# Layer 0's attention loop in another order: single scores beside maxima's products, products with v in two pieces, a spread finish, roots on VectorE

## The reference

```python
# layer 0, attention: 16 heads of 8
qkv = x @ W_attn + b_attn
att = einsum('bhtd,bhsd->bhts', q, k) / sqrt(8) + alibi_causal_mask   # -inf above the diagonal
y = einsum('bhts,bhsd->bhtd', softmax(att), v)
return y @ W_proj + b_proj
# layer 0, FFN: x normalised again, scaled by its largest magnitude, times ternary weights
xq = clip(xn * 128 / gamma, ...);  return (xq @ w_q) * (gamma * beta / 128)
# layer 1: linear attention with RoPE in chunks, and an FFN with a gate over 8 experts
xn = layernorm(x)
```

## Time and profile before

| | us |
|---|---|
| median of 3 runs | 527.51 (521.96 to 528.45) |
| the profiled execution | 526.21 |
| its span, first to last instruction | 524.4 |

### The profile page before, as it was taken

The page is one execution under the profiler, slowest core; times in us unless marked ns, Lnnn a source line. Parts: engine busy times, 40 slices in busy tenths (PEclk is TensorE's granted clock), DMA queues, the critical chain, the costliest instruction groups (busy, mean ns, idle before and its releaser), DMA issues. The chain is left out here.

```text
span 524.4 us, 10855 instructions
## 1 busy us (share of the span) xinstructions
PE 423.6 (81%) x4220; PEld 192.8 (37%) x4220; DVE 352.3 (67%) x584; ACT 273.4 (52%) x599; POOL 183.5 (35%) x277
## 2 busy tenths in 40 slices
PE   6796788887887877777779689796789868987995
PEld 3253212222232222222233254243446534644764
DVE  5778758788787977787625468498644964586361
ACT  1565367777767777767746702345603340344331
POOL 3013413445230313232210106566623851486220
PEclk9998769999999999999979779798989998999999
DMA  7643060424202002020000003131020301120000
GB/s 230 195 113 70 28 216 0 150 69 165 70 3 69 2 22 49 2 68 2 3 3 0 2 36 131 54 122 63 2 81 21 123 12 71 41 101 2 2 22 21
DMA packets 19094, 31.92 MB, mean 61 GB/s; under 512 B 2544, under 2 KB 7120, under 8 KB 18724
## 3 DMA queue, kind: packets, MB, share of 16 engines
q1 hardware_dynamic: 19044, 31.23, 18.6%
HBM read 13.20 MB, written 8.06 MB: 41 GB/s over the span
## 5 line engine op out<-in xcount | busy, mean ns | idle before, releaser
L1103 DVE TENSOR_REDUCE pmax<-PS 128x8 f32<-128x1024 f32 x144 | 171.9, 1222 | 50.2 <-PE PS L597 32.0
L1414 ACT ACTIVATE prob<-PS 128x512 f32<-128x512 f32 (+1 forms) x320 | 159.9, 552 | 74.1 <-PE PS L665 70.9
L1558 POOL TENSOR_SCALAR_AFFINE_SELECT prob<-prob 128x512 f32<-128x512 f32 x64 | 39.9, 635 | 180.3 <-ACT prob L1414 180.3
L665 PE MATMUL PS<-q_op,k_op 55*128 55x512 bf16 (+3 forms) x384 | 61.6, 341 | 43.7 <-ACT prob L1414 41.3
L683 PE MATMUL PS<-prob,vaug 128*16 128x512 f32 (+3 forms) x768 | 83.1, 523 | 0.0
L597 PE MATMUL PS<-k_op,q_op 52*128 52x128 bf16 (+3 forms) x576 | 58.6, 280 | 10.0 <-DVE pmax L1103 5.4
L665 PEld LDWEIGHTS PS<-q_op,k_op 55*128 55x128 bf16 x384 | 18.4, 94 | 124.8 <-ACT prob L1414 108.7
L1596 POOL TENSOR_TENSOR xn<-state,c_sb 128x512 f32<-128x512 f32 x28 | 32.1, 1146 | 71.8 <-DVE state L1284 63.1
L792 PE MATMUL PS<-xnT,w_sb 128*128 128x512 f32 x80 | 45.6, 672 | 11.7 <-DVE by_sin L1251 11.7
L1284 DVE TENSOR_TENSOR state<-PS,xn 128x512 f32<-128x512 f32 x28 | 19.3, 688 | 40.7 <-PE PS L875 27.8
L1579 POOL TENSOR_TENSOR qr<-qr,turned 128x512 f32<-128x512 f32 x32 | 42.9, 1359 | 5.0 <-DMA turned<-by_sin 5.0
(11 more groups left out here) (182 smaller groups left out, 536.3 us busy)
## 6 DMA issues: line engine op xcount, KB each, us to landing
turned<-by_sin SPq DMA_DIRECT2D x80, 128.0 KB, 2.0
k_op<-k_scr SPq DMA_DIRECT2D x14, 220.0 KB
q_op<-q_scr SPq DMA_DIRECT2D x14, 208.0 KB
...
```

What stands on the lines that cost most here:

```text
L665: last = mm(PS[:, (GH * s + h) % ST_BANKS, at:at + nn], k_op[rows, slot, h // 2, P * j:P * j + P], q_op[rows, slot, h // 2, P * i0:P * i0 ...
L1103: vec.tensor_reduce(pmax[:, of_pair, at:at + step * (TPS - 1) + 1:step], both.rearrange("p a (b c) -> p a b c", c=P), AX.X, ALU.max).then_ ...
L1414: sca.activation(prob[:, s % P_SLOTS, h, 0:UNIT_W[u]], PS[:, k % ST_BANKS, 0:UNIT_W[u]], ACT.Exp).then_inc(s_exp, 1)
L1558: po.affine_select(out=blk, in_=blk, compare_op=ALU.is_ge, fill=0.0, base=0, pattern=[[0, GH], [1, P]], channel_multiplier=-1).then_inc(s_ ...
```

## The change

1. The loop's half steps take one head's score at a time, and beside each, on the other rows of PE, one half of a max item (`max_beside`) where the half step's first item is one. The odd item of a step with three goes to the first half.
2. `pv(s - 1)` is cut in two pieces: the first, without own blocks, after the third score, the second, with the own blocks, after the fourth; only the second waits for POOL.
3. `ROUNDS` has longer rounds (12 products in place of 18 for a head). Own blocks are now in 5 of 9 rounds, and the mask is added by four products of 64 rows by 64 columns of the array, over the own blocks alone. `ROW` shrinks from 6 to 4.
4. ACT copies `yacc` between the third and the fourth exponential of the step after.
5. yt, yT and the first proj go into groups 5 to 7 (`MIDWAY`): steps 42, 45, 49, 52 (yt), 56, 59 (yT) and 68 (proj); proj(1), back, back and xn1T are in steps 71, 72, 73 and 76. `quantise` is in steps 63 and 65.
6. The roots of layer 1's norm are taken on DVE (`inverse_root`: 16 small operations, a first guess by an integer shift and four rounds of Newton's method) in place of ACT's Sqrt, in step 74 and in layer 1's chunk 1.

```diff
-ORDER = [(0, 1, 3, 2), (6, 7, 5, 4)]
-DIAGONALS = {0: ORDER[0], 3: ORDER[1]}
-ROUNDS = [[(i, i, 1, at) for at, i in enumerate(DIAGONALS[0])],
-          [(1, 0, 1, 0), (3, 0, 3, 1)], [(2, 0, 2, 0), (6, 4, 2, 2)],
-          [(i, i, 1, at) for at, i in enumerate(DIAGONALS[3])],
-          [(7, 0, 4, 0)], [(7, 4, 3, 0), (5, 0, 1, 3)], [(5, 1, 4, 0)], [(4, 0, 4, 0)], [(6, 0, 4, 0)]]
-
-ROW = [6, 8]
-ROWS_AT = [0, 6 * TPS]
-
-PLACE = {0: (3, 6), 1: (11, 1), 2: (22, 1), 3: (27, 9), 4: (32, 1), 5: (37, 1), 6: (41, 1), 7: (48, 1), 8: (28, 1)}
+def pv_pieces(segs):
+    j, i0, nn = segs[0]
+    if i0 != j:
+        return [[(j, i0 + m * nn // 2 // P, nn // 2, m * nn // 2)] for m in range(2)]
+    return [[(j, i0 + 1, nn - P, P)], [(j, i0, P, 0)] + [(j1, i1, n1, nn) for j1, i1, n1 in segs[1:]]]
+
+
+PIECES = [pv_pieces(segs) for _, segs in UNITS]
+
+
+
+ORDER = [(3, 2, 0, 1), (5, 6, 4, 7)]
+ROUNDS = [[(3, 0, 4, 0)], [(2, 0, 3, 0), (0, 0, 1, 3)], [(1, 0, 2, 0), (5, 4, 2, 2)],
+          [(7, 0, 4, 0)], [(7, 4, 4, 0)], [(6, 0, 4, 0)], [(5, 0, 4, 0)], [(4, 0, 4, 0)], [(6, 4, 3, 0), (4, 4, 1, 3)]]
+
+OWN = [[at + i - j for i, j, nb, at in pieces if i < j + nb] for pieces in ROUNDS]
+
+ROW = [4, 8]
+ROWS_AT = [0, 4 * TPS]
+
+PLACE = [0, 5, 14, 40, 44, 24, 18, 33, 29]
 NR, NR0 = len(ROUNDS), 3
 NMAX = NR * PAIRS
 MAX_OF = [(p, r) for rs in (range(NR0), range(NR0, NR)) for p in range(PAIRS) for r in rs]
...
-TAIL = [(70, "yt", 0, 0), (71, "yt", 0, 1), (72, "yt", 1, 0), (73, "yt", 1, 1), (74, "yT", 0, 0), (74, "yT", 1, 0),
-        (75, "proj", 0, 0), (75, "proj", 1, 0), (76, "back", 0, 0), (76, "back", 1, 0), (79, "xn1T", 0, 0)]
+TAIL = [(71, "proj", 1, 0), (72, "back", 0, 0), (73, "back", 1, 0), (76, "xn1T", 0, 0)]
+MIDWAY = {(5, 5): ("yt", 0, 0), (5, 11): ("yt", 0, 1), (6, 0): ("yt", 1, 0), (6, 6): ("yt", 1, 1),
+          (6, 12): ("yT", 0, 0), (7, 0): ("yT", 1, 0), (7, 17): ("proj", 0, 0)}
 
 
 def item_stream():
...
+            if (n, u) in MIDWAY:
+                out.append(MIDWAY[n, u])
             if n == NG and u in (13, 15):
                 out.append((("lanes", "spread")[u == 15], 0, 0))
...
-QUANTISE_STEP = [72, 73]
+QUANTISE_STEP = [63, 65]
...
             pe.wait_ge(s_pick, 32)
             pe.wait_ge(s_masks, 16)
 
+            def max_ready(k):
+                _, n, u = ITEMS[k]
+                slot = n % OP_SLOTS
+                pair, r = MAX_OF[u]
+                if n == 0 and r == 0:
+                    for w_, it in enumerate(ITEMS):
+                        if it[0] == "prep" and it[2] // 2 == pair:
+                            used(pe, w_)
+                elif u == 0:
+                    pe.wait_ge(s_op[slot], OP_EACH * (n // OP_SLOTS + (slot > 0)))
+
+
+            def max_piece(k, t, odd):
+                _, n, u = ITEMS[k]
+                slot, ring = n % OP_SLOTS, 3 + 2 * (k % 2)
+                pair, r = MAX_OF[u]
+                i, j, nb, at = ROUNDS[r][t]
+                rows = rows_of(odd, MAX_K)
+                return mm(PS[:, ring + odd, P * at:P * (at + nb)], q_op[rows, slot, pair, P * i:P * i + P],
+                          k_op[rows, slot, pair, P * j:P * (j + nb)], start=(t == 0), stop=(not OWN[r]),
+                          skip_group_check=True)
+
+            def max_done(k, last):
+                _, _, u = ITEMS[k]
+                ring = 3 + 2 * (k % 2)
+                own = OWN[MAX_OF[u][1]]
+                if own:
+                    cols = slice(own[0], own[-1] + 1, max(1, own[-1] - own[0]))
+                    for h in range(2):
+                        for odd in range(2):
+                            rows = slice(HALF * odd, HALF * odd + HALF)
+                            ps = PS[HALF * h:HALF * h + HALF, ring + odd, :].rearrange("p (b c) -> p b c", c=P)
+                            last = mm(ps[:, cols, :], ident_b[rows, rows],
+                                      causal_b[rows, h:h + 1, :].broadcast_to([HALF, len(own), P]),
+                                      start=False, stop=True, skip_group_check=True)
+                last.then_inc(s_item, 1)
+
+
+
+            def max_beside(k, odd):
+                if odd:
+                    used(pe, k - 2)
+                    max_ready(k)
+                for t in range(len(ROUNDS[MAX_OF[ITEMS[k][2]][1]])):
+                    last = max_piece(k, t, odd)
+                if not odd:
+                    max_done(k, last)
+
...
                     last.then_inc(s_item, 1)
                 elif kind == "max":
-                    slot = n % OP_SLOTS
-                    pair, r = MAX_OF[u]
-                    if n == 0 and r == 0:
-                        for w_, it in enumerate(ITEMS):
-                            if it[0] == "prep" and it[2] // 2 == pair:
-                                used(pe, w_)
-                    elif u == 0:
-                        pe.wait_ge(s_op[slot], OP_EACH * (n // OP_SLOTS + (slot > 0)))
-                    for t, (i, j, nb, at) in enumerate(ROUNDS[r]):
+                    max_ready(k)
+                    for t in range(len(ROUNDS[MAX_OF[u][1]])):
                         for odd in range(2):
-                            rows = rows_of(odd, MAX_K)
-                            last = mm(PS[:, ring + odd, P * at:P * (at + nb)], q_op[rows, slot, pair, P * i:P * i + P],
-                                      k_op[rows, slot, pair, P * j:P * (j + nb)], start=(t == 0), stop=(r not in DIAGONALS),
-                                      skip_group_check=True)
-                    for odd in range(2 if r in DIAGONALS else 0):
-                        last = mm(PS[:, ring + odd, :].rearrange("p (b c) -> p b c", c=P), ident_b,
-                                  causal_b.rearrange("p (o c) -> p o c", o=1).broadcast_to([P, TPS, P]),
-                                  start=False, stop=True, skip_group_check=True)
-                    last.then_inc(s_item, 1)
+                            last = max_piece(k, t, odd)
...
-            def pv(s):
+            def pv(s, piece):
                 n, u = divmod(s, NU)
                 b, g = GROUPS[n]
-                half, segs = UNITS[u]
-                pe.wait_ge(s_exp, GH * (s + 1))
-                pe.wait_ge(s_tri, TRI[s])
-                if u in (0, 3):
-                    pe.wait_ge(s_acc, 1 + 2 * n + (u == 3))
-                at = 0
-                for j, i0, nn in segs:
+                half = UNITS[u][0]
+                if piece == 0:
+                    pe.wait_ge(s_exp, GH * (s + 1))
+                    if u in (0, 3):
+                        pe.wait_ge(s_acc, 1 + 2 * n + (u == 3))
+                else:
+                    pe.wait_ge(s_tri, TRI[s])
+                for j, i0, nn, at in PIECES[u][piece]:
                     c0 = P * i0 - SPAN * half
                     for h in range(GH):
                         last = mm(PS[STRIP * h:STRIP * h + VW, 7, c0:c0 + nn], vaug[:, TPB * b + j, g * GH + h, :],
-                                  prob[:, s % P_SLOTS, h, at:at + nn], start=(j == 0),
+                                  prob[:, s % P_SLOTS, h, at:at + nn], start=(j == 0 and piece == 0),
                                   stop=(u in (2, 9)), skip_group_check=True)
-                    at += nn
-                last.then_inc(s_pv, 1)
+                if piece:
+                    last.then_inc(s_pv, 1)
 
             def unit_b(k, part):
 
...
             for s in range(NSTEP + 1):
                 beside = items_of_step(s) if s < NSTEP else ()
                 for half in range(2):
-                    if s < NSTEP:
-                        scores(s, range(GH // 2 * half, GH // 2 * (half + 1)))
-                    for k in (beside[:len(beside) // 2], beside[len(beside) // 2:])[half]:
+                    mine = (beside[:(len(beside) + 1) // 2], beside[(len(beside) + 1) // 2:])[half]
+                    with_scores = s < NSTEP and mine and ITEMS[mine[0]][0] == "max"
+                    for odd in (1, 0):
+                        if s < NSTEP:
+                            scores(s, [GH // 2 * half + 1 - odd])
+                        if with_scores:
+                            max_beside(mine[0], odd)
+                        if s and half:
+                            pv(s - 1, 1 - odd)
+                    for k in mine[1:] if with_scores else mine:
                         item(k)
-                if s:
-                    pv(s - 1)
 
 
             pe.wait_ge(s_exp, GH * NSTEP)
...
+            def inverse_root(t, eps):
+                y, half = rstd[:, t], std[:, t]
+                aux = rstd2[:, t]
+                note(vec.tensor_scalar(half, mv[:, t, 1], eps, -0.5, ALU.add, ALU.mult))
+                link(vec.tensor_scalar(aux, mv[:, t, 1], eps, None, ALU.add))
+                link(vec.tensor_scalar(y.bitcast(I32), aux.bitcast(I32), 1, None, ALU.logical_shift_right))
+                link(vec.tensor_scalar(y.bitcast(I32), y.bitcast(I32), -1.0, float(0x5F3759DF), ALU.mult, ALU.add))
```

(14 more changed lines are left out.)

46 lines of the change are left out of this document (26 added, 20 removed).

## The result

| | before | after |
|---|---|---|
| median, us | 527.98 (521.96 to 529.21) | 536.26 (534.24 to 539.23) |
| ratio | | 1.021 (95%: 1.015 to 1.027) |
| the profiled execution; its span | 526.21; 524.4 | 536.07; 534.3 |

The change makes the kernel 2.1% slower. The forecast was 511.2 us with a range of 500 to 525, and 0.06 for slower; it was wrong.

What follows compares the result with a forecast made beforehand. No engine is full; two chains of transfers in each group of ten steps limit the loop's gain. Terms -1.6 - 2.5 - 1.8 - 0.8 + 1.9 - 11.9 - 1.0 + 2.7 = -15.0 from 526.2 gave 511.2 us, range 500 to 525.

Steps and rivals of the forecast that it cites:

- loop order: Attention loop, single scores beside maxima and product in two pieces: free full step 2.5 us against 2.76, 0.35 us a group gained.
- the second item's ring: Attention loop step, second max item's buffer from one reduction's end to the next, first piece inside: 2.52 us a step.
- u5 to u8: Sixth to ninth steps of each group of ten in the attention loop: claimed nothing gained, PE only standing longer, 1.8 us.
- Load chain: From a group's sixth step to the next group's first maxima, transfers then operand loads: stays 12.24 us, PE stands 1.8.
- half chain: Second and third steps of each group, mrow copy and four small transfers: together stay about 6.0 us, gain 0.
- The moved items: yt, yT, proj and quantise moved from the last group into steps 42 to 68: +1.9 us in sum, four of them 0.
- The last group: Steps 70 to 79 and the loop's end: 41.5 us down to 29.6, gain 11.9; at upper ends 32, gain 9.5.
- Start: First steps of the loop: -1.6 us in step 1 and -2.5 in steps 3 to 9.
- The clock behind the loop: After the attention loop: with half of PE's stand before 295.97, less time at the lower clock, -1.0 us.
- B: Rival: PE's longer stands before loads lower the clock once or twice more in the loop; 523 us, chance 0.16.
- C: Rival: the clock falls at the load stand in every group; 538 us, slower than before; chance 0.06.
- D: Rival: second item's chain in a loop step longer than worked out, steps of 3.05 us; 521 us, chance 0.08.

## Why the prediction was wrong, by its own steps

**The step that failed first: loop order.** It put the second item's ring at 2.52 us with the piece in it, and set that against the old step, 2.76, as a gain. Measured is 0.06 + 0.32 + 0.56 + 0.45 + 1.22 = 2.61. That small miss is not the point; two others are. The masks belong in this ring, and I had put them to PE's busy time alone (0.15 to 0.2 us): 0.24 us where they cover two blocks (204.98 to 205.22 in the rows below). The steps with own blocks take 2.75 to 2.86. And the number that mattered was not asked for: the ring without the piece. It is 0.56 shorter, DVE becomes the bound, and the steps u5 to u8 take 2.45 to 2.68. I compared the new step with the old one, and never the edit with its absence. Forecast for the order was a gain; measured, the pieces' place alone costs 3.0 us in steps 10 to 39, 6.6 in 40 to 69 and 18 of the whole.

```profile
204.98 0.30 PE L616 MATMUL PS<-masks_sb 64*64 64x256 bf16 x4
205.08 0.60 ACT L1490 ACTIVATE prob<-PS 128x512 f32<-128x512 f32 x1 [0.32 <-PE PS L713]
205.22 0.41 PE L732 MATMUL PS<-prob,vaug 128*16 128x128 f32 x8
```

**What hides the loop's gain.** Load chain and half chain were the forecast's reason for 0.35 us a group. In the kernel after the load chain bound nothing (0.3 us of k_op waits where I had 1.8 in each group); the steps with own blocks, at 2.75 to 2.86, were no faster than before. In the kernels with fast steps the stands did come, 0.9 to 1.8 us in step 19, but with the product at the end the loop gained 4.2 us in three groups in spite of them, not 0.35 a group. So this part was right in kind and too strong.

**The moved items.** "Within the chains' slack: 0" for four of them, +1.9 in all. Measured 8.7 in the kernel after, and 4.2 in the kernel before. With the load chain not binding there was no slack in the kernel after. And the price of one is more than its 1.03 us of PE: it stands in front of scores and takes a ring buffer. In the kernel without pieces the same items cost 6.2.

**The last group** was right in mechanism: PE's stand for xn 1.79 us (forecast 1.7), the whole 27.7 to 29.3 us in the five kernels with single scores and at most 3.4 us at half clock there (29.6), 31.8 in the profile shown, with 10.2 us at half clock: step 76 took 6.94 in place of 5.03 (4.7). But against 36 to 41 us without the moved items, what it gives is what the loop paid.

**Start**: -4.1 forecast, +0.8 measured, with 27 us at half clock in it (20 before), which the forecast had let stay. Part is the pieces again: with 17 us at half clock in each, 41.2 with them between the scores, 37.7 to 39.3 without, and 40.9 for the kernel before with its items moved. The rest goes with the clock, and why that stayed low longer is open.

**The yacc copy**: the forecast had ACT idle 0.7 us before it and late at u1. Shown, 0.42 in step 50 and up to 1.0; its place costs 1.1 us in three groups, about half of the 0.65 a group that the forecast had it late by.

**Layer 1's root**: 3.1 us for the operations (3.2 to 3.8) and 2.4 for PE (2.7). The mechanism and the price were right. The whole lost 6 to 8 us by it; that the clock is the rest, 3 us and more, is likely and not shown, and it was not in the forecast.

**The clock behind the loop**: forecast -1.0. It had been read off one stand that got shorter. Measured mean 0.91 in place of 0.95, and 7.7 us for the stretch, 2.4 of them the root's.

**The rivals.** B and C had the clock fall in the loop, at loads. It did so once, behind the 1.79 us of the kernel with the first piece ahead; behind stands for k_op of 0.9 to 1.6 us in other kernels it did not. In the kernel after it was low in steps 0 to 9, behind step 76 and in layer 1. D, the longer chain of the second item, was the nearest in mechanism. I gave it 0.08 and thought that u5 to u8 would hide it.

**A likeness that is luck.** With both pieces and the copy at the end the ratio is 0.977, and with ACT's root as well 0.974, near the 0.969 of the forecast. That does not bear it out: there the loop gains more than forecast (4.2 against 1.9 us in steps 10 to 39) and the moved items cost more (6.2 against 1.9).
